# The state-space stage: product, scan and weighting for both channel halves at once

## The reference

```python
dt = softplus(Bm @ dt_w + dt_b)
def step(hst, inp):
    xt, dtt, Bt, Ct = inp
    dA = exp(dtt[..., None] * A)
    hst = hst * dA + dtt[..., None] * Bt[:, None, :] * xt[..., None]
    yt = sum(hst * Ct[:, None, :], -1)
    return (hst, yt)
y = (y + D_skip * xs) * silu(gate)
return y @ out_w + res
```

## Time and profile before

| | us |
|---|---|
| median of three runs | 4698.73 |
| lowest, highest | 4696.16, 4699.51 |
| the profiled execution | 4698.96 |
| its span | 4697.2 |
| the state-space stage, first instruction to last | some 590 of these, from 3043.9 to 3630.9 |
| VectorE busy in the stage's turn from 3288 to 3355 | 64.2 of 67.0 |

### The profile page before, as it was taken

One profiled execution on the slowest core, in us unless ns is written; L12 is line 12 of the kernel. 1 busy time (PEld: TensorE's weight loads), 2 busy tenths in 40 slices (PEclk: granted clock), 3 DMA queues, 4 the chain that ended last, 5 costly groups with the idle time before them and its releaser, 6 DMA issues. The chain is left out here.

```text
span 4697.2 us, 90969 instructions
## 1 busy us (share of the span) xinstructions
PE 3784.2 (81%) x25828; PEld 2709.6 (58%) x25828; DVE 3316.0 (71%) x9072; ACT 2369.2 (50%) x5659; POOL 2399.8 (51%) x3960
## 2 busy tenths in 40 slices
PE   7888799779999879778878977468776788779875
PEld 5666566756666556566655657423322566456565
DVE  7888688456666678656557875569998665478756
ACT  3444466455555556544445554545554454246545
POOL 5666554434333445446653554367776564035543
PEclk9999899889999989888988998789989899989988
DMA  6000233200000033233313322212221331033223
GB/s 253 0 0 0 83 114 110 74 23 1 0 1 0 9 124 126 72 114 110 106 66 125 122 83 64 73 50 64 64 61 52 118 115 66 0 120 121 86 61 91
DMA packets 244140, 343.48 MB, mean 73 GB/s; under 512 B 26672, under 2 KB 186816, under 8 KB 242688
## 3 DMA queue, kind: packets, MB, share of 16 engines
q1 hardware_dynamic: 230528, 310.64, 20.0%
q0 software_dynamic: 13184, 27.81, 1.7%
HBM read 183.42 MB, written 148.64 MB: 71 GB/s over the span
## 5 line engine op out<-in xcount | busy, mean ns | idle before, releaser
L1218 POOL TENSOR_TENSOR wb_prob<-wb_prob,wb_rden 128x128 f32<-128x128 f32 (+1 forms) x512 | 248.2, 506 | 377.9 <-DVE wb_rden L1395 377.5
L793 DVE TENSOR_REDUCE l0att_rowmax<-l0att_S 128x2 f32<-128x512 f32 x512 | 340.3, 686 | 88.4 <-PE l0att_S L1026 81.8
L793 DVE TENSOR_REDUCE l1ffn_rowmax<-l1ffn_S 128x2 f32<-128x512 f32 x512 | 341.4, 685 | 80.8 <-PE l1ffn_S L1026 75.3
L2094 POOL TENSOR_TENSOR ssm_hc<-core_AW_all,ssm_Cs 128x512 f32<-128x512 f32 x256 | 321.1, 1270 | 129.7 <-DVE core_AW_all L2240 96.0
L1260 ACT ACTIVATE wb_prob<-wb_biased,wb_nmax 128x128 f32<-128x128 f32 (+1 forms) x512 | 228.6, 447 | 252.9 <-DVE wb_nmax L1388 250.0
L1691 POOL DMA_INDIRECT results<-e_y,e_back x220 | 211.0, 959 | 270.2 <-DVE e_y L1818 171.3
L2339 PE MATMUL ssm_Y<-ssm_hc,core_ident 128*128 128x512 f32 x512 | 288.1, 673 | 56.0 <-POOL ssm_hc L2094 29.6
L1026 PE MATMUL l1ffn_S<-l1ffn_K,l1ffn_Q 128*128 128x512 f32 x512 | 252.0, 496 | 82.5 <-DVE l1ffn_rowmax L793 47.1
L1026 PE MATMUL l0att_S<-l0att_K,l0att_Q 128*128 128x512 f32 x512 | 256.0, 503 | 72.9 <-DVE l0att_rowmax L793 42.3
L2240 DVE TENSOR_TENSOR_SCAN core_AW_all<-core_AW_all,ssm_U 128x512 f32<-128x512 f32 x256 | 310.3, 1212 | 0.8 <-ACT core_AW_all L2183 0.8
L2183 ACT ACTIVATE core_AW_all<-ssm_dt,ssm_A 128x510 f32<-128x510 f32 x256 | 178.5, 716 | 221.5 <-DVE core_AW_all L2240 219.8
(11 more groups left out here) (509 smaller groups left out, 11502.6 us busy)
## 6 DMA issues: line engine op xcount, KB each, us to landing
bounce<-l0att_parts SPq DMA_DIRECT2D x128, 256.0 KB
bounce<-l1ffn_parts SPq DMA_DIRECT2D x128, 256.0 KB, 2.8
ssm_Cs<-c_rows SPq DMA_DIRECT2D x128, 256.0 KB, 3.0
routed<-core_Y SPq DMA_DIRECT2D x8, 2176.0 KB, 26.0
l0att_Q<-bounce SPq DMA_DIRECT2D x128, 128.0 KB
l0att_K<-bounce SPq DMA_DIRECT2D x128, 128.0 KB
bounce<-l1att_parts SPq DMA_DIRECT2D x64, 256.0 KB
l1ffn_Q<-bounce SPq DMA_DIRECT2D x128, 128.0 KB
```

The source lines that it names most:

```text
L793: dve.tensor_reduce(out=rowmax[:, jp, qt, 2 * pair:2 * pair + 2], in_=S[a % 2][:].rearrange("p (j k) -> p j k", j=2)[:, :, 0:keys(qt)], op ...
L1218: ins = pool.tensor_tensor(out=prob[:, w_ % NP, a:b], in0=prob[:, w_ % NP, a:b], in1=rden[:, w_ % NP, n:n + 1].to_broadcast([P, b - a]), o ...
L2094: pool.tensor_tensor(out=hc[:, u % 4], in0=hs[:, u % 4], in1=Cs[:, n % 4], op=ALU.mult)\
```

## The change

Both channel halves of a state are now one instruction on VectorE and on POOL: a product of 1024 columns, a scan of 1024 columns, a weighting of 1024 columns. ScalarE's decays and TensorE's sums stay halves. BU is one buffer over two PSUM banks (the two that were there before), so the product of a state stands directly ahead of its scan and waits for the scan before. The rings dA, hs and hc hold three states (six halves) where they held four halves; `hs` has its own memory. The semaphores of the merged steps count states. The tables of VectorE and POOL count states: `power`, `split`, `dt` and `du` stand behind the same weightings as before; statistics, gate and apply stand one half later than before and add where it was. The tables of ScalarE and TensorE are as they were.

```diff
-        BU = [ps("U0"), ps("U1")]
+        BU = ps("U", (P, CT * T2))
...
-        DVE_AT = {0: "stats", 2: "gate", 4: "apply", 7: "add"}
-        POOL_AT = {1: "power", 19: "split", 25: "dt", 27: "du"}
+        DVE_AT = {0: "stats", 1: "gate", 2: "apply", 3: "add"}
+        POOL_AT = {0: "power", 9: "split", 12: "dt", 13: "du"}
...
+        RING = 3
+        dA = core.AW_all[:, 0:RING * CT * T2].rearrange("p (b c t) -> p b c t", b=RING, c=CT)
+        hs = sb("hs", [P, RING, CT, T2])
...
+            def weigh(u):
                 pool.wait_ge(scanned.sem, u + 1)
-                if w_ % CT == 0:
-                    pool.wait_ge(c_sent[n % 4].sem, 16 * (n // 4 + 1))
-                await_(pool, summed, u - 3)
-                pool.tensor_tensor(out=hc[:, u % 4], in0=hs[:, u % 4], in1=Cs[:, n % 4], op=ALU.mult)\
+                pool.wait_ge(c_sent[u % 4].sem, 16 * (u // 4 + 1))
+                await_(pool, summed, CT * (u - RING + 1))
+                pool.tensor_tensor(out=hc[:, u % RING], in0=hs[:, u % RING],
+                                   in1=Cs[:, u % 4, None, :].to_broadcast([P, CT, T2]), op=ALU.mult)\
                     .then_inc(hc_made.sem, 1)
...
-                await_(act, scanned, u - 3)
-                act.activation(both(dA[:, u % 4])[:, :, 1:L], both(dt[:, r % 2, c])[:, :, 1:L], ACT.Exp,
+                if c == 0:
+                    await_(act, scanned, u - RING + 1)
+                act.activation(both(dA[:, u % RING, c])[:, :, 1:L], both(dt[:, r % 2, c])[:, :, 1:L], ACT.Exp,
                                scale=A[:, c, n:n + 1]).then_inc(dA_made.sem, 1)
...
-                await_(dve, scanned, u - 1)
-                dve.tensor_tensor(out=BU[u % 2][:], in0=du[:, r % 2, c], in1=BB[n % 2][:], op=ALU.mult)\
+                dve.wait_ge(b_made.sem, u + 1)
+                await_(dve, scanned, u)
+                dve.tensor_tensor(out=BU[:].rearrange("p (c t) -> p c t", c=CT), in0=du[:, r % 2],
+                                  in1=BB[u % 2][:, None, :].to_broadcast([P, CT, T2]), op=ALU.mult)\
                     .then_inc(bu_made.sem, 1)
...
             def scan(u):
+                dve.wait_ge(dA_made.sem, CT * (u + 1))
+                await_(dve, hc_made, u - RING + 1)
                 dve.wait_ge(bu_made.sem, u + 1)
-                dve.wait_ge(dA_made.sem, u + 1)
-                await_(dve, hc_made, u - 3)
-                dve.tensor_tensor_scan(hs[:, u % 4], dA[:, u % 4], BU[u % 2][:], 0.0, ALU.mult, ALU.add)\
+                dve.tensor_tensor_scan(hs[:, u % RING].rearrange("p c t -> p (c t)"),
+                                       dA[:, u % RING].rearrange("p c t -> p (c t)"), BU[:], 0.0, ALU.mult, ALU.add)\
                     .then_inc(scanned.sem, 1)
...
-                        if u == 0:
-                            inflow(0)
-                        if u + 1 < TURNS * WS:
-                            inflow(u + 1)
-                        scan(u)
+                        inflow(r * N + n)
+                        scan(r * N + n)
```

64 lines of the change are left out of this document (29 added, 35 removed).

## The result

| | before | after |
|---|---|---|
| median | 4698.73 us (5 runs beside those of after) | 4723.55 us (5 runs) |
| lowest, highest | 4689.77, 4703.93 | 4717.36, 4730.27 |
| after / before | | 1.0058, 95% interval 1.0041 to 1.0075 |
| the profiled execution, its span | 4698.96, 4697.2 | 4720.43, 4718.7 |
| the state-space stage | 3043.9 to 3630.9: 587.0 us | 3047.1 to 3654.2: 607.1 us |

The change makes the kernel slower by 0.6%. The forecast was 4706, with a range up to 4717: it had the sign, and too little of it. The profiled execution is 21.5 us longer, and 20.1 us of that is the stage.

The account below looks back on a forecast made before the run. VectorE was taken to set the pace of the state-space stage. The terms summed to -0.6 (last turn) + 5.6 (seven turns at +0.8 us) + 1.9 (tail) = +6.9 us, giving 4706 us, with a range from 4688 to 4717.

Parts of the forecast that it names:

- Term 1, VectorE's work: VectorE's merged product and scan: a state takes 3.74 us against 3.775, a gain of 0.6 us a turn.
- The rival of cheap links: Waiting for the VectorE instruction just ahead costs nothing extra: a state costs 3.34 us, the kernel 4679; chance 0.13.
- Term 2, B(8): POOL's longer product makes TensorE 0.83 us later; VectorE stalls 0.1 us for state 8's B rows, before 0.62.
- Term 3, ScalarE's decays: VectorE's scans wait for decays queued behind SiLU and the logarithm: 1.7 us at state 9, 0.4 at state 13.
- Term 4: Tail: the gate starts 4.5 us after the last scan, +1.9 us once; at the other places nobody waits.
- The rival of the clock: TensorE's clock falls ahead of x0 (convolution taps), making each turn 6.7 us longer: +47 us, 4753; chance 0.08.
- no lateness: TensorE's sum ahead of the convolution taps is not late, so no added stalls: 4696 us; chance 0.12.
- the long scan saves nothing: VectorE's merged scan takes 2.42 us, no fixed cost saved: +10 us, 4716; chance 0.12.

Follow-up runs that it names:

- eps_on_pool: Changed kernel with POOL's product in halves, apply directly behind the gate, ScalarE's pieces moved, epsilon added by POOL: 4674.10 us, 0.9960 of before.
- before_two_moves: Kernel before with the apply directly behind the gate and the epsilon added by POOL, ScalarE's table unmoved: 4679.84 us, 0.9974 of before.
- silu_later: Changed kernel with ScalarE's SiLU moved behind the decay of half 19 in place of half 17: 4724.23 us (one run).
- silu_log_later: Changed kernel with SiLU behind the decay of half 19 and the logarithm behind that of half 27: 4709.24 us, 1.0044 of before.
- apply_behind_gate: Changed kernel with VectorE's apply moved from behind state 2 to directly behind the gate of state 1: 4700.22 us, 1.0020 of before.
- inflow_in_sbuf: Changed kernel with the product u*B written to SBUF instead of PSUM, so the scan reads both operands from SBUF: 4831.29 us (one run).

## Why the prediction was wrong

The prediction had the sign, and the mechanism and size of the waits. Of a regular turn it missed 1.4 us (2.23 in place of 0.8), and 1.2 of these stand in work that it took for unchanged. Step by step:

- **Term 1, VectorE's work**: a state takes 3.75 to 3.76 us (forecast 3.74): product to scan 1.36, scan to product 2.39, both links 0.1 as taken. Held. The rival of cheap links is out. The rule behind it, in "VectorE: DVE Perf Modes" of the Trainium skill, section "The DRAIN you can't avoid", that the semaphore costs nothing extra, is not borne out by these rows: before, a scan starts 0.09 us ahead of its neighbour's end, here every one starts 0.10 to 0.13 behind it. No run takes the semaphores away, so how much of that is theirs stays open. The gain in a regular turn is 0.45 us (forecast 0.6), and by eps_on_pool against before_two_moves 0.4; in the last turn it is only 0.1, a difference that was not taken apart.
- **Term 2, B(8)**: forecast 0.1, measured 0.23 beyond the link. Held within 0.2 us.
- **Term 3, ScalarE's decays**: forecast 1.7 and 0.4, measured 1.68 and 0.34 beyond the link; silu_later and silu_log_later showed them to be a matter of queue order. Terms 2 and 3 together gave +1.48 a turn where the sum had +1.4. Held.
- **Term 4, and in it the failed step**: "At the other places (stats, gate, apply and add of the turn before ...) nobody waits." Nobody waits there, true, but two of these pieces got longer. The sum put the change of VectorE's other work, 6.7 us a turn by the rival of cheap links, at nothing without a reason. The apply went from 2.04 to 3.12 us and the epsilon instruction from 1.12 to 1.24, 1.2 us in a regular turn, 8.2 us in the seven by the groups above. The signs of it stood in the trace of before: the apply's four instructions had a median of 334 ns and a longest of 1330, POOL's product length, and an instruction of four columns took 1124 ns where its shortest was 170. apply_behind_gate shows the block for the apply, inflow_in_sbuf for a scan. The tail itself was as forecast up to the gate, and 1.6 us shorter behind it.
- **The rival of the clock** was given 0.08 as all or nothing: 47 us if it decided, nothing if not. It came in part, in two turns of seven and in x0's passes only: 3.7 us in the profiled execution, up to five of seven turns in other kernels. Its price per turn was 1.8 us, not 6.7.

With 1.48, 1.20 and -0.45 a turn, 0.6 for tail and start-up and 3.7 for the clock, the same sum comes to 4719. The measured median is 4.6 us above that: 1.4 lie outside the stage in the profiled execution, and 3.1 are the median of the five over the profiled one; neither is explained. Without the block's 8.2 us the median would be 4715, inside the range, without the clock's 3.7 it would be 4720, still outside. So the block is what puts the result outside the range. With both gone the sum is 4707: that this lies so near the forecast is in part luck, since the tail was 1.7 us cheaper than forecast and the gain of term 1 smaller. The rivals "no lateness" and "the long scan saves nothing" are out by the waits and by 2287 ns.

## What to carry to other kernels

When an engine's instructions are made longer, ask not only who waits for their results, but which instructions of the *other* engine cannot run at the same time. Look for it in the spread of durations, not in the waits: one form of instruction whose longest case equals the length of a POOL instruction is probably being held by it (move it to where POOL is idle, and see), and the profile calls that busy. Such instructions (VectorE from SBUF to SBUF with two inputs, or the layer norm's scale and shift) belong where POOL is idle by construction, for example behind a gate whose operand is in PSUM; and an operand in PSUM kept the hot scan here free of POOL.

A merge can pay on the engine that sets the pace, here 0.4 us a turn, and a merged instruction waits for the last of its inputs: every piece that stands between the two halves' producers becomes a wait. Split a change by engines and try the parts; here one part was nearly neutral and the other the loss.

## What the runs showed of the hardware that I had not expected

- An instruction of 128 x 4 values, which takes 170 ns with POOL idle (the like instruction of line 1852 at 3006.82), took 1.24 us beside products of 2.35 us and 1.80 us beside two products of 1.27 us back to back. It stood through the start of the second one when it had come 0.5 us ahead of it, and not when it came 0.2 us ahead: POOL's next instruction can keep what the first one held, and smaller POOL instructions are no sure remedy.
- A scan with both inputs in SBUF lost 0.83 us a state to POOL, 97.5 us of scan time in the kernel; the same scan with one input in PSUM lost nothing: all 128 of the changed kernel took 2286 to 2289 ns.
- Eight more passes ahead of x0 made its passes slow in more turns, not fewer, at a granted clock of 0.60 in the stretch with x0.
